# Streams: another order of work on VectorE, TensorE and ScalarE, and the three gate parts of a chunk in one step

## The reference

```python
h = shift_token(x); q, k, v = split(h @ wqkv)        # 8 heads of 64
q = l2norm(q) * qs; k = l2norm(k) * ksc; q, k = rotary_xpos(q, k)
o = local_attention(q, k, v)                          # windows of 64 tokens, own and previous
x = x + o @ wo
h = layernorm(shift_token(x)) @ w1 + b1               # 128 -> 2 x 341
a, g = split(h)
x = x + (a * gelu(g)) @ w2 + b2
```

## Time and profile before

| | |
|---|---|
| median of 3 runs | 1581.75 us (1580.46 to 1586.36) |
| the profiled execution | 1587.68 us |
| its span | 1585.8 us |
| PE busy | 1431.8 us, 90% of the span |
| DVE busy | 1356.6 us, 86% |
| ACT busy | 1227.6 us, 77% |
| POOL busy | 894.4 us, 56% |
| mean clock granted to TensorE | 0.977 of full speed |

### The profile page before, as it was taken

One profiled execution on the slowest core, in us unless ns is written; L12 is line 12 of the kernel. 1 busy time (PEld: TensorE's weight loads), 2 busy tenths in 40 slices (PEclk: granted clock), 3 DMA queues, 4 the chain that ended last, 5 costly groups with the idle time before them and its releaser, 6 DMA issues.

```text
span 1585.8 us, 46462 instructions
## 1 busy us (share of the span) xinstructions
PE 1431.8 (90%) x18975; PEld 1120.9 (71%) x18975; DVE 1356.6 (86%) x1692; ACT 1227.6 (77%) x1834; POOL 894.4 (56%) x626
## 2 busy tenths in 40 slices
PE   5999997899999999999998757899999999999998
PEld 3777874777777777777776444677777777777776
DVE  6777757889999999999995866999999999999994
ACT  4876867678888888888885757688888888888884
POOL 3333005666666666676661645666666666766761
PEclk9999998999999999999999878999999999999999
DMA  4313003665665656657651003656656566665652
GB/s 120 107 47 97 4 7 72 126 120 118 114 125 121 121 115 123 121 116 122 128 96 28 0 7 69 128 123 120 121 123 120 118 120 123 119 122 122 115 103 73
DMA packets 359855, 157.46 MB, mean 99 GB/s; under 512 B 299410, under 2 KB 335836, under 8 KB 359644
## 3 DMA queue, kind: packets, MB, share of 16 engines
q1 hardware_dynamic: 359644, 154.51, 49.3%
HBM read 27.29 MB, written 6.29 MB: 21 GB/s over the span
## 4 chain that ended last, share of the span: by engine, by line
DVE 33%; ACT 23%; PE 19%; issue 11%; DMA 5%; POOL 5%; SPq 4%; DVEq 0%; ACTq 0%; POOLq 0%
DVE t L1270 9%; DMA t<-t 5%; POOL t L1436 4%; DVE t L1277 4%; DVE t L1289 4%; ACT t L1072 4%; DVE t L1254 3%; ACT t L1143 3%; PE PS L199 3%; PE PS L201 2%; DVE t L1323 2%; PE PS L200 2%; ACT t L1059 2%; ACT L1196 2%; ACT L1143 2%
## 5 line engine op out<-in xcount | busy, mean ns | idle before, releaser
L1430 POOL TENSOR_TENSOR t<-t 128x1024 f32<-128x1024 f32 x128 | 309.1, 2415 | 235.6 <-DVE t L1260 233.5
L1436 POOL TENSOR_TENSOR t<-t 128x512 f32<-128x512 f32 x256 | 319.5, 1270 | 147.8 <-DVE t L1270 147.5
L1270 DVE TENSOR_TENSOR t<-t 128x1024 f32<-128x1024 f32 x128 | 277.8, 2171 | 0.1
L1059 ACT ACTIVATE t<-PS 128x1024 f32<-128x1024 f32 x128 | 131.9, 1031 | 71.7 <-PE PS L201 71.6
L1277 DVE TENSOR_TENSOR t<-t,PS 128x1024 bf16<-128x1024 f32 x128 | 155.8, 1217 | 36.9 <-ACT PS L1079 36.9
L852 PE MATMUL PS<-t 128*64 128x65 f32 x4096 | 148.4, 225 | 41.9 <-DVE t L1323 40.0
L199 PE MATMUL PS<-wqh,HH 128*128 128x512 f32 x384 | 167.3, 436 | 18.6 <-DVE t L1260 16.0
L852 PEld LDWEIGHTS PS<-t 128*64 128x64 f32 x4096 | 130.6, 138 | 58.5 <-DVE t L1323 49.5
L1072 ACT CAST t<-t 128x1024 bf16<-128x1024 f32 x128 | 133.4, 1042 | 42.4 <-POOL t L1436 42.2
L1289 DVE TENSOR_REDUCE t<-PS 128x8 bf16<-128x1024 f32 x128 | 155.6, 1216 | 10.9 <-PE PS L801 10.9
L1254 DVE TENSOR_REDUCE t<-t 128x16 f32<-128x1024 f32 x128 | 154.3, 1206 | 7.5 <-ACT t L1059 7.4
(11 more groups left out here) (242 smaller groups left out, 3389.6 us busy)
## 6 DMA issues: line engine op xcount, KB each, us to landing
t<-t SPq DMA_DIRECT2D x254, 130.0 KB, 2.3
t<-turns SPq DMA_DIRECT2D x128, 128.0 KB, 2.8
t<-yT SPq DMA_DIRECT2D x108, 128.0 KB, 2.3
t<-t SPq DMA_TRANSPOSE x304, 3.3
t<-in_c_rope SPq DMA_DIRECT2D x32, 128.0 KB, 2.2
turns<-t SPq DMA_DIRECT2D x32, 128.0 KB, 2.1
t<-in_L_attn_a_x SPq DMA_DIRECT2D x4, 512.0 KB, 6.7
t<-yT SPq DMA_DIRECT2D x16, 127.8 KB, 3.2
```

The costliest lines, as they stand in the source:

```text
L1270: e.e.tensor_tensor(BL.ta[i % 2].rearrange("p (x h) d -> p x h d", x=2), BL.qn.rearrange("p (x h) d -> p x h d", x=2), cos.to_broadcast([1 ...
L1430: e.e.tensor_tensor(BL.tc.rearrange("p (x h) d -> p x h d", x=2), BL.qn.rearrange("p (x h) d -> p x h d", x=2), sin.to_broadcast([128, 2, ...
L1436: e.e.tensor_tensor(tv[:, :, 32 * s:32 * s + 32], tv[:, :, 32 * s:32 * s + 32], BL.tc[:, :, 32 * (1 - s):32 * (1 - s) + 32], ALU.add).then ...
```

## The change

Four things are changed, all in the streams.

1. VectorE: `normed(s-1)` stands ahead of `divide(s-4)`. In steps of kind 3 `reduce_maxima` stands ahead of `add_out`.
2. TensorE: `project(s)` stands ahead of `turn_result(s-4)` and `feed_bank_6`. In steps of kind 3 `project_out` stands behind `maxima`, as it did already in kind 1.
3. The gates: for all chunks but the last two of a stack, gate part 2 is computed in kind 3 with the other two, in bank 7; part 1 goes to bank 5 by the new `feed_bank_5`. ScalarE takes them out in the order 0, 1, `copy_values`, 2. The wait of `gather` in kind 0 for gate part 2 goes away, and that of kind 3 is for part 2.
4. ScalarE: `rnorms(s)` stands ahead of `gelus`. In steps of kind 0 `high` and `high_there` of tile s-1 stand right behind the gelus, ahead of the load of the exponential table; the next step (kind 1) leaves them out.

```diff
+        def last_gate(C):
+            return 2 if C < NC - 2 else 1
...
 (project_out)
+                if chunk_at(i + 4, 11) is not None:
+                    e.wait_ge(S.ff_ev, evicted(u, chunk_at(i + 4, 11), 1))
...
 (fed_banks_free)
                 if chunk_at(s, 11) is not None:
-                    e.wait_ge(S.ff_ev, evicted(u, chunk_at(s, 11), 1))
-                if chunk_at(s, 12) is not None:
-                    e.wait_ge(S.ff_ev, evicted(u, chunk_at(s, 12), 2))
+                    e.wait_ge(S.ff_ev, evicted(u, chunk_at(s, 11), last_gate(chunk_at(s, 11))))
...
+            def feed_bank_5(s):
+                C = chunk_at(s, 11)
+                if C is not None and C < NC - 2:
+                    e.wait_ge(S.la_e, hi(s - 3) + 1)
+                    first(C, 1, 1, 5, S.ff_g)
...
 (TensorE)
+                if on(0):
+                    project(s)
                 if on(4):
                     turn_result(s - 4)
                 feed_bank_6(s)
-                if on(0):
-                    project(s)
+                feed_bank_5(s)
...
-                late = chunk_at(s, 9) is not None
+                late = chunk_at(s, 9) is not None or chunk_at(s, 11) is not None
...
 (ScalarE)
-                if on(2):
+                if on(2) and chunk_at(s, 13) is None:
                     high(s - 2)
-                if on(2):
                     high_there(s - 2)
...
-                if chunk_at(s, 12) is not None:
-                    gate(chunk_at(s, 12), 2, 6)
...
+                if chunk_at(s, 11) is not None and chunk_at(s, 11) < NC - 2:
+                    gate(chunk_at(s, 11), 0, 6)
+                    gate(chunk_at(s, 11), 1, 5)
                 if on(2):
                     copy_values(s - 2)
-                if chunk_at(s, 11) is not None:
+                if chunk_at(s, 11) is not None and chunk_at(s, 11) < NC - 2:
+                    gate(chunk_at(s, 11), 2, 7)
+                elif chunk_at(s, 11) is not None:
                     gate(chunk_at(s, 11), 0, 6)
                     gate(chunk_at(s, 11), 1, 7)
+                if on(0):
+                    rnorms(s)
                 if chunk_at(s, 12) is not None:
                     gelus(chunk_at(s, 12), range(3))
+                    if on(1):
+                        high(s - 1)
+                        high_there(s - 1)
                     e.e.preload_act_table_set("natural_log_exp_and_others")
-                if on(0):
-                    rnorms(s)
...
 (VectorE)
+                if on(1):
+                    normed(s - 1)
                 if on(4):
                     divide(s - 4)
-                if on(1):
-                    normed(s - 1)
...
+                if on(2) and chunk_at(s, 11) is not None:
+                    reduce_maxima(s - 2)
                 if on(4):
                     add_out(s - 4)
...
-                if on(2):
+                if on(2) and chunk_at(s, 11) is None:
                     reduce_maxima(s - 2)
```

More of the change, by code:

```diff
@@ L921, in feed_bank_6 @@
                     first(chunk_at(s, 11), 0, 1, 6, S.ff_g)
-                if chunk_at(s, 12) is not None:
-                    first(chunk_at(s, 12), 2, 1, 6, S.ff_g)
                 if chunk_at(s, 13) is not None:
@@ L936, in feed_bank_7 @@
                 if chunk_at(s, 11) is not None:
-                    first(chunk_at(s, 11), 1, 1, 7, S.ff_g)
+                    first(chunk_at(s, 11), last_gate(chunk_at(s, 11)), 1, 7, S.ff_g)
                 if chunk_at(s, 16) is not None:
```

## The result

The change makes the kernel slower: 1595.29 us, the median of 6 runs (1588.69 to 1598.82), against 1581.42 us for the kernel before (6 runs); the ratio is 1.0084, 95% interval 1.0068 to 1.0100. The forecast was 1576 us and no measurable change. The time lies inside the stated range of 1553 to 1600 us, but above the 1589.7 us up to which the prediction spoke of no change: the kernel went the other way.

The account below looks back on a forecast made before the run. VectorE was taken to bound kinds 1 and 2, while TensorE never rests in kinds 3 and 0. Steady periods gave -3.5 us and early steps -2.4, together about -6: 1576 us against the median, range 1553 to 1600.

Parts of the forecast that it names:

- VectorE: On VectorE, `normed` ahead of `divide` lets `divide` run beside GpSimd's sine product, giving back 0.86 us a step, 3.4 a period.
- The last rival: On VectorE, `divide` waits for GpSimd: +1.25 us a step in at least two of four, +60 us, 1642; chance 0.02.
- Where the waits stand: On TensorE, 0.8 us ahead of `values` in kind 1; kind 2's scores still wait for a DMA; period 36.0 to 36.8.
- The sum: Four steps of 8.70, 9.42, 9.48 and 8.69 us make a period of 36.29 against 36.53, -0.24 a period.
- the 0.1 given back: Taken off the gain per period, in us, for semaphores the chains leave out, leaving -0.15 x 24 = -3.5 us.
- Kind 3: TensorE, scores to scores: one gate part more, three matmuls at 0.23 us, +0.69, from 8.01 to 8.70.
- Kind 0: TensorE, scores to scores: loses the gate part, -0.69, waits for `copy_result`, about +0.24; from 9.87 to 9.42 us.
- Kind 2: Chain from scores through project, transposes, copy, squares, product and gather: 8.69 us, before 8.74.
- Kind 1: Chain through ScalarE, 0.8 us wait ahead of `values`, transposes ending it at 18.9: lasts 9.48 us, before 9.91.
- Steps outside the steady periods: Steps without feed-forward work: VectorE's cycle shrinks to 7.26 us from 7.98; some 12 steps, -0.2 each on average, -2.4.
- The slower one: Kind 2's slack is gone: transposes landing later than counted lengthen the period to 37.1, 1593 us; chance 0.22.
- TensorE's full gain: On TensorE: other chains don't bind, period falls to about 34.9, -43 us, 1538; half gives 1560; chance of some such case 0.22.

Follow-up runs that it names:

- e3: The kernel after, with `turn_result` and `feed_bank_6` put back ahead of `project` on TensorE: 1638.50 us, ratio 1.0350.
- e5: The kernel before, with only `normed` ahead of `divide` and `project` ahead of `turn_result` and `feed_bank_6`: 1591.44 us, ratio 1.0058.
- e7: The kernel after, with `squares` ahead of `copy_result` on ScalarE and the gate parts as in the kernel before: 1561.64 us, ratio 0.9876.
- e1: The kernel before, with only `normed` ahead of `divide` on VectorE: 1667.01 us, ratio 1.0534.
- e9: The kernel before, with only `squares` ahead of `copy_result` on ScalarE: 1655.67 us, ratio 1.0457.
- e6: The kernel after, with only `squares` ahead of `copy_result` on ScalarE in every step: 1578.98 us, ratio 0.9994.
- e12: The kernel of e7, with `divide` put back ahead of `normed` on VectorE: 1639.42 us, ratio 1.0359.

## Why the prediction was wrong

**VectorE: right.** `divide` ran beside GpSimd's product at no cost, the rotation product still ends 4.76 us behind the start of `normed`, and VectorE's busy time fell from 34.41 to 32.31 us a period. The last rival is out.

**Where the waits stand: right but for one.** The exponentials start 13.24 us behind the scores of kind 0, forecast 13.12; TensorE waits for them ahead of `values`, 0.59 us where 0.8 was forecast; kinds 3 and 0 have no rest; kind 3 is longer. But the scores of kind 2 do not wait for a transpose, and the period of 37.04 lies outside the 36.0 to 36.8 that the prediction gave as its own limit.

**The sum: wrong, by 0.74 us a period** (36.29 against 37.03, before the 0.1 given back). The step that failed is the sizing of TensorE's own row of work: one spacing of 0.23 us for all large matmuls, a moved `project_out` that costs nothing, and a project in kind 2 that can start 1.47 us behind the scores. From scores to scores, in us; "before" is the usual period:

| kind | before | forecast | measured | measured less forecast |
|---|---|---|---|---|
| 3 | 8.00 | 8.70 | 8.96 | 0.26 |
| 0 | 9.89 | 9.42 | 9.51 | 0.09 |
| 1 | 9.38 | 9.48 | 9.60 | 0.12 |
| 2 | 9.26 | 8.69 | 8.96 | 0.27 |

TensorE's timeline after, from the maxima's subtraction (L838) to the transposes, and the end of kind 3:

```profile
446.38 0.62 PE L838 MATMUL PS<-idb,t 128*128 128x128 bf16 x8
446.81 0.48 PE L199 MATMUL PS<-wqh,HH 128*128 128x512 f32 x1
447.13 0.40 PE L200 MATMUL PS<-wql,HH 128*128 128x512 f32 x1
447.36 0.39 PE L201 MATMUL PS<-wqh,HL 128*128 128x512 f32 x1
...
448.27 0.60 PE L864 MATMUL PS<-cst,t 128*128 128x128 f32 x4
448.63 0.47 PE L199 MATMUL PS<-HH,w1h 128*114 128x512 f32 x1
448.94 0.40 PE L200 MATMUL PS<-HL,w1h 128*114 128x512 f32 x1
...
451.26 0.40 PE L201 MATMUL PS<-HH,w1l 128*113 128x512 f32 x1
451.58 0.41 PE L800 MATMUL PS<-mk,eye 64*64 64x512 bf16 x4
451.82 0.39 PE L805 MATMUL PS<-t 64*64 64x128 bf16 x16
452.15 1.16 PE L877 MATMUL PS<-t,wo 128*128 128x128 f32 x8
453.23 1.15 PE L856 MATMUL PS<-t 128*64 128x65 f32 x32
```

The first of the large matmuls takes 0.32 us behind bf16 ones (446.81 to 447.13) and 0.31 behind the transposes (448.63 to 448.94); one that follows its own kind takes 0.23. Before, the transposes stood right behind the bf16 matmuls and project in one row with the others, so this was paid once; now twice. That is 0.09 us a step that the forecast left out, about 0.07 of it net, since the bf16 matmuls ahead make room 0.03 sooner. So:

- Kind 3, 0.26: this, and 0.19 at its end. The last projection is followed by a bf16 matmul after 0.32 instead of 0.23, and `project_out` keeps the gather waiting for 1.08 where it held up the maxima for 0.98.
- Kind 0, 0.09: mostly this.
- Kind 2, 0.27: project starts at 438.03 instead of 437.85, as `normed` isn't done (0.18), and takes 1.49 instead of 1.38.
- Kind 1, 0.12: the forecast let the transposes end it, 18.9 us behind the scores of kind 0. They ended no wait; the way through `values`, for which it had 18.62, took 19.11. The exponentials were 0.12 later, and from `values` to the scores TensorE took 4.79 us instead of 4.47, again by changes of kind and by `project_out`.

That the neighbours' kind is the cause rests on spacings, in this trace and in e3, where the same matmul of project has other neighbours and takes 0.23 again. Busy time alone would not show it: it is 34.98 us a period on average before, 35.53 in e5, 35.68 in e7 and 36.00 after, but also 35.65 in e1 and 35.85 in e9, where TensorE's order is that of before.

**The period that was read was not a usual one.** The prediction's rows hold a wait of 0.45 us for a transpose, at 438.38. Such a wait comes in 6 of the 24 periods before. Two periods on, the scores of kinds 1 and 2 follow each other without it, after 9.38 us:

```profile
465.35 0.39 PE L816 MATMUL PS<-eye,mk 64*128 64x512 bf16 x2
474.73 0.39 PE L816 MATMUL PS<-eye,mk 64*128 64x512 bf16 x2
```

So the 9.91 us of kind 1 and the "rest" of 8.74 for kind 2 are 9.38 and 9.26 in a usual period. By the kinds' usual lengths the forecast makes kind 1 longer, not shorter, and kind 2 is where time is won. The 34.47 busy us of TensorE, cut at `normed`, come from the same late landing: 34.98 is the average, which leaves 1.55 us to gain and not 2.06.

**Steps outside the steady periods.** Over tiles 0 to 12 and 64 to 76 the profiled execution gained 1.4 and 4.6 us, where 2.4 in all was forecast. But the period with the first gelus of each stack took 40.22 and 40.61 us instead of 36.52 and 36.97, 7.3 together, which the prediction had not seen. In that step TensorE has no second product to do, and meets the whole chain through ScalarE: it waits 2.26 us for the exponentials (2.65 in the second stack) instead of the 0.59 of the later periods, and a lower clock behind that wait costs another 1.5 us, as the last section shows. The other 22 periods make 10.2 us more. What is left of the 10.2 us between the two spans, -1.3 us, lies outside these stretches and was not followed.

**The rivals.** The slower one named 1593 us and a period of 37.1, which is nearly what came, but by another mechanism: late transposes, which end no wait in the kernel after. That the time fell into the stated range, which took this rival in, is luck. What it had right is that kind 2 lost its slack: there the chain project, transposes, copy, squares, product now ends in a wait of 0.45 us. TensorE's full gain was barred by the copy ahead of the squares, which the prediction named as a term (3.97 us) and didn't follow further. With that order changed (e6) the period is 36.36, and with the gates as before too (e7) 35.83, a gain of 0.70 where TensorE waited 1.55 us before. The rest isn't waiting any more, since TensorE is then busy for 35.68.

## What to carry to other kernels

Where engines run hand-written lists and meet at every step, the lists are one order, not four: of seven combinations of three exchanges, the single ones cost 2.6 to 3.1 us of 36.5 and all three together gained 0.6. Before moving an instruction ahead on one engine, find on every other engine the pair that waits for it in the old order, and move that too. Here a wait on the loop that closes in each step was paid in each step (2.78 us of waits for 3.03 of period in e12), although VectorE and ScalarE had slack on average. And look at several periods before reading one: the one read here was the exception in four.

## What the runs showed of the hardware

TensorE's spacing of 512-column matmuls differed by what came before: 0.23 us behind one of its kind, 0.31 to 0.32 behind bf16 matmuls or fp32 transposes, and 0.34 for the first one behind a wait (431.61 to 431.95 after). VectorE's product of a PSUM and a broadcast SBUF operand took 0.69 us beside GpSimd's (410.95 before, 438.12 after) as well as alone (401.69 before). And in the kernel after, TensorE waited 2.26 us in the first step with gelus. Its granted clock was 1.00 in the stretch with that wait and 0.75 in the next 6.76 us; within these, from 358 to 360, it was 0.50, the lower of the two levels (1.2 GHz), and by 361 it was full again:

```profile
349.69:355.90 6.21, 4.04 (x71) 3.14 (x67) 4.29 (x6) 6.08 (x9) 2.89 (x2) 1.00 0.46 98
355.90:362.66 6.76, 6.67 (x80) 4.93 (x82) 4.06 (x6) 3.98 (x8) 2.52 (x2) 0.75 0.52 107
358.00:360.00 2.00, 2.00 (x23) 0.94 (x22) 1.35 (x2) 1.88 (x5) 0.59 (x1) 0.50 0.24 50
```

The matmuls from the feed of bank 7 to the start of the gather took 3.95 us there (357.26 to 361.21), and 2.44 at full clock (432.87 to 435.31): 1.5 us more. The second stack repeats it, with 2.65 us of waiting, a granted clock of 0.50 behind it and 3.93 us for these matmuls. But in the same steps of e7 TensorE waited 1.8 and 2.4 us and the clock stayed at 1.00, so these runs don't show that the length of the wait alone decides.
